# Weighted sums of a window attention for two pairs at a time, in slots 1 and 3 of a quad

## The reference

```python
xw  = windows(roll(norm(x)))                       # 7 x 7 windows: 49 tokens of 96
q, k, v = split(xw @ qkv_w + qkv_b)                # 12 heads of 8; layer 3: 4 heads of 24
attn = softmax(q * hd**-0.5 @ k.T + bias + mask)   # over 49 keys
out = (attn @ v) @ proj_w + proj_b                 # attn @ v: the weighted sums
x   = x + unroll(unwindows(out))
x   = x + mlp(norm(x))
```

## Time and profile before

| | |
|---|---|
| median of 3 runs | 7,912.68 us (7,911.06 to 7,913.54) |
| profiled execution, its own time | 7,913.45 us |
| its span, first to last instruction | 7,911.6 us |
| mean granted TensorE clock | 0.991 |
| busy TensorE / VectorE / ACT / GpSimd | 96% / 77% / 63% / 67% |

### The profile page before, as it was taken

The page is one execution under the profiler, slowest core; times in us unless marked ns, Lnnn a source line. Parts: engine busy times, 40 slices in busy tenths (PEclk is TensorE's granted clock), DMA queues, the critical chain, the costliest instruction groups (busy, mean ns, idle before and its releaser), DMA issues.

```text
span 7911.6 us, 312040 instructions
## 1 busy us (share of the span) xinstructions
PE 7632.4 (96%) x109686; PEld 5869.5 (74%) x109686; DVE 6090.9 (77%) x18297; ACT 5020.8 (63%) x8745; POOL 5284.7 (67%) x6553
## 2 busy tenths in 40 slices
PE   5999999999999999999999999999999999999998
PEld 4777777777777777777777777777777777777777
DVE  6877778767787877877878687786787878778677
ACT  3847657557784765745777475674577747567457
POOL 4956657567795765756789476675678857566566
PEclk9999999999999999999999999999999999999999
DMA  2101101010010110101011011010101101011010
GB/s 61 39 11 30 51 13 32 12 35 18 24 40 30 34 47 17 32 8 41 11 31 46 23 33 42 22 33 7 43 5 36 57 11 33 13 27 30 11 41 25
DMA packets 309910, 227.60 MB, mean 29 GB/s; under 512 B 217380, under 2 KB 305767, under 8 KB 306345
## 3 DMA queue, kind: packets, MB, share of 16 engines
q1 hardware_dynamic: 307858, 215.98, 10.2%
q10 hardware_dynamic: 1622, 6.13, 0.2%
HBM read 117.62 MB, written 104.37 MB: 28 GB/s over the span
## 4 chain that ended last, share of the span: by engine, by line
PE 80%; DVE 7%; issue 6%; DVEq 2%; POOL 2%; ACT 1%; POOLq 0%; ACTq 0%
PE ps L942 13%; PE ps L992 12%; PE ps L917 10%; PE ps L893 10%; PE ps L1035 8%; PE ps L1008 8%; PE ps L949 5%; PE ps L972 5%; PE ps L982 3%; PE ps L926 3%; DVE xn L1210 2%; DVE bst L1061 2%; PE ps L1022 2%; PE ps L873 1%; DVE x L1366 1%
## 5 line engine op out<-in xcount | busy, mean ns | idle before, releaser
L667 POOL TENSOR_TENSOR S<-S,mx 113x588 f32<-113x588 f32 (+1 forms) x2048 | 2066.8, 1009 | 1075.2 <-DVE mx L1261 1069.8
L773 ACT ACTIVATE S<-S 113x588 f32<-113x588 f32 (+1 forms) x2048 | 1251.5, 611 | 480.0 <-POOL S L667 465.3
L1259 DVE TENSOR_TENSOR S<-ps,bias 113x588 f32<-113x588 f32 (+1 forms) x1536 | 969.6, 631 | 611.5 <-PE ps L917 568.5
L1261 DVE TENSOR_REDUCE mx<-S 113x12 f32<-113x588 f32 (+1 forms) x2048 | 1359.6, 664 | 70.8
L802 ACT ACTIVATE PT<-ps 123x490 f32<-123x490 f32 (+1 forms) x2048 | 1059.4, 517 | 399.8 <-PE ps L992 395.2
L992 PEld LDWEIGHTS ps<-turn,S 113*123 113x123 f32 (+2 forms) x8704 | 1006.6, 158 | 386.2 <-issue 185.4
L1008 PEld LDWEIGHTS ps<-w,G 128*98 128x98 f32 x12288 | 1152.0, 168 | 158.9 <-issue 87.5
L992 PE MATMUL ps<-turn,S 113*123 113x113 f32 (+2 forms) x8704 | 1232.6, 266 | 13.7 <-ACT S L773 4.5
L1008 PE MATMUL ps<-w,G 128*98 128x96 f32 (+1 forms) x12288 | 1152.8, 250 | 0.0
L1035 PE MATMUL ps<-h,w 97*128 97x392 f32 x3072 | 1125.3, 503 | 9.1 <-ACT G L837 9.1
L942 PEld LDWEIGHTS ps<-Va,PT 123*49 123x49 f32 (+1 forms) x18432 | 815.4, 125 | 292.7 <-issue 243.9
(11 more groups left out here) (94 smaller groups left out, 11984.3 us busy)
## 6 DMA issues: line engine op xcount, KB each, us to landing
v_between<-Vd SPq DMA_DIRECT2D x384, 165.4 KB
Va<-v_between SPq DMA_DIRECT2D x768, 41.3 KB
Vb<-v_between SPq DMA_DIRECT2D x768, 27.6 KB
v_between<-Vd SPq DMA_DIRECT2D x128, 153.1 KB
Vl<-v_between SPq DMA_DIRECT2D x256, 76.6 KB
out_dram<-x SPq DMA_DIRECT2D x15, 1176.0 KB
x<-x_dram SPq DMA_DIRECT2D x14, 1176.0 KB
mask<-mask_dram SPq DMA_DIRECT2D x258, 37.5 KB
```

The costliest lines, as they stand in the source:

```text
L667: pool.tensor_tensor(v, v, m, ALU.subtract).then_inc(a_sub, 1)
L773: act.activation(S[:, e, 0:nh * N], S[:, e, 0:nh * N], ACT.Exp).then_inc(a_exp, 1)
L1259: dve.tensor_tensor(dst, scores, b, ALU.add).then_inc(a_bi, 1)
L1261: dve.reduce_max(mx[:, e, 0:nh], S[:, e, 0:n].rearrange("p (h k) -> p h k", k=N), axis=AX.X).then_inc(a_mx, 1)
```

## The change

The weighted sums become a function `weigh(par, pairs)`. TensorE calls it in slot 3 for pairs 0 and 1 of quad i, behind the waits for the weights of pair 1 (before: pair 0), the scaled output of quad i - 1 and the values; and in slot 1, after the queries, for pairs 2 and 3 of quad i - 1, behind the wait for the weights of its pair 3. Slots 0 and 2 have none. On VectorE the scaling moves from slot 2 to slot 1, and the four `bn_stats` from slot 1 to slot 3, right ahead of the four `bn_aggr`. The line of the value copy is not changed: it stays in slot 2, where the scaling stood ahead of it.

```diff
+                    def weigh(par, pairs):
+                        pieces = [blocks_of(nh, par, w) for w in range(2)]
+                        for p in pairs:
+                            for b in range(blocks):
+                                for w in range(2):
+                                    rows, _, h, v = pieces[w][b]
+                                    v = v[:, :, p]
+                                    out = Ops[ROW2 * w:ROW2 * w + N, p, h:h + v.shape[1], :]
+                                    last = pe.matmul(out, PT[0:rows, p, b, N * w:N * (w + 1)], v,
+                                                     start=(nh == 4 or b % 2 == 0), stop=True, skip_group_check=True)
+                        return last
...
-                        if on(-1) if s < 3 else on(0):
-                            wait(a_pte, i.pair(s - 3))
-                            p = (s + 1) % 4
-                            if s == 3:
-                                wait(a_o, i - 1)
-                                spread = spread_count(l, g, i, t)
-                                pe.wait_ge(s_vb[t], spread if i.static else pe.snap(spread))
...
-                            if s == 2:
-                                last.then_inc(a_pv, 1)
+                        if s == 3 and on(0):
+                            wait(a_pte, i.pair(1))
+                            wait(a_o, i - 1)
+                            spread = spread_count(l, g, i, t)
+                            pe.wait_ge(s_vb[t], spread if i.static else pe.snap(spread))
+                            weigh(t, (0, 1))
...
                         if s == 1 and on(1):
                             wait(a_res, i - 2)
                             project(queries_at(l, i), 0).then_inc(a_q, 1)
+                        if s == 1 and on(-1):
+                            wait(a_pte, (i - 1).pair(3))
+                            weigh(o, (2, 3)).then_inc(a_pv, 1)
...
-                        if s == 2 and on(-1):
+                        if s == 1 and on(-1):
                             wait(a_pv, i - 1)
...
-                        if s == 1 and on(-2):
+                        if s == 3 and on(-2):
                             wait(a_res, i - 2)
                             if not (i.static and i.index < 4):
                                 wait(a_mv, i - 4)
                             stats(i - 2, xb, (i - 2).index * QUAD, QUAD, t, a_bn)
-                        if s == 3 and on(-2):
                             aggregate(i - 2, QUAD, t, a_bn, a_agg)
```

## The result

The changed kernel takes 8,049.35 us (median of 4 runs, 8,047.37 to 8,053.61) where the kernel before takes 7,913.08: 136 us more, a ratio of 1.0173 [1.0156, 1.0191]. The forecast was 8,014, within 7,905 to 8,085. Part 1 of the page of the changed kernel, busy time, share of the span and instructions, against the earlier trace rows: TensorE has the same number of matmuls, and is busy for a smaller share of a longer span.

The account below looks back on a forecast made before the run. TensorE, busy nearly throughout, with pair 1's transposes waiting for their exponential, was taken as the bound. Per-quad terms 0.25 + 0.26 + 0.26 + 0.10, times 29 quads and 4 groups, gave +101 us: 8,014 us, range 7,905 to 8,085.

Parts of the forecast that it names:

- The late ST(3): Slot 0, layers 1 and 2: transposes of pair 3's exponentials wait 0.29 us because of GpSimd's power; +0.26 us per quad.
- The faster rival: Pair 3's exponential is ready in time, as GpSimd or ACT work 0.3 us sooner: 7,873 us; chance 0.12.
- Layer 0: ACT's xn delays pair 3's exponential, so its transposes wait; net +0.42 and +0.07 in the two quads, mean +0.25 us.
- slots 1 and 2 stay at 4.96 us together: Layers 1 and 2: pair 1's transposes still wait for their exponential, so these slots change by nothing.
- Entering the group from the projection: Slot 1: going from query projection to weighted sums costs 0.08 us, between nothing and 0.16.
- Layer 3: Slot 0's output projection waits for ACT's eviction of its input, taken at 0.18 us; +0.10 us per quad.
- a rival for layers 0 to 2 only: Slot 3's statistics and aggregation delay pair 0's add and the residual; the query projection waits: 8,084 us; chance 0.12.
- 0.28 us of cover: Slot 1: the query projection starts 3.25 us after pair 0's scores start, the residual ends at 2.97; no wait.
- VectorE's moves, costed at nothing: Scaling to slot 1, statistics to slot 3: no instruction added or removed; pair 0's add perhaps a tenth late, covered.
- The tie of the scaling: Scaled product ends about 3.5 us after pair 1's scores start, pair 2's scores end at 3.4; costed at nothing.
- The rule on drains: TensorE: mode changes per quad fall from 13 to 12, an estimated 41 us saved, some 7,872 us.
- One reading of the prediction: Kernel before, GpSimd: pair 3's subtraction starts at 712.32, where the power ends, not where its maximum lets it.

Follow-up runs that it names:

- the move of xn: Changed kernel with ACT making xn behind pair 3's exponential instead of ahead of it in layer 0: 8,020.13 us, 1.0136.
- The exchange of order: Changed kernel with slot 1's weighted sums of pairs 2 and 3 ahead of the query projection on TensorE: 8,001.54 us, 1.0113.
- the first experiment: Changed kernel with GpSimd's copy, sum and power behind pair 1's subtraction (slot 1) instead of pair 2's in layers 1 and 2: 8,015.86 us, 1.0131.

## Why the prediction was right, and where its size was off

- **The late ST(3) in layers 1 and 2**: right in its place, cause and size. Slot 0 was forecast at 2.8 and is 2.83; the wait was forecast at 0.29 and is 0.28. That GpSimd's power causes it is shown: with it elsewhere slot 0 is 2.48. The faster rival, that GpSimd would take that work sooner, did not happen.
- **Layer 0**: the waits were forecast at 0.45 and 0.10 (0.57 less a margin of 0.47), and are 0.47 and 0.12. Shown by the move of xn.
- **The mis-sized term: "slots 1 and 2 stay at 4.96 us together".** They take 5.07 in layers 0 to 2. Entering the group from the projection was priced well (0.85 from queries to weighted sums, 705.62 to 706.47, against 0.76 from queries to transposes in the kernel before, 705.81 to 706.57, and as much behind scores in layer 3 of the kernel with the groups in slots 0 and 2: 0.09). What was not priced is the exit: until then no ST stood right behind weighted sums, and ST(0) now runs 0.10 longer there. Slot 2, freed of its group, hides nothing any more, so the 0.10 goes on through ACT's eviction and pair 1's exponential to ST(1). 0.11 x 87 quads x 4 groups = 38 us, which is the whole gap between 8,014 and 8,049 and a little more. The exchange of order, which brings back 4.97 and 4.31, shows the cause.
- **Layer 3**: the wait for the output projection's input is 0.18, as taken. The wait for the residual, which the prediction priced as a rival for layers 0 to 2 only, is real here in every second quad: 0.22, or 0.11 per quad. Slot 3 gives 0.06 back (+0.18 where +0.24 was forecast), so +0.15.
- **"0.28 us of cover" for the query projection** was rightly computed from the residual's old time, but hung on the wait itself. Without the late ST(3) the cover is gone, and the first experiment met that. The forecast of the faster rival, 7,873, was wrong for this reason too.
- **VectorE's moves, costed at nothing**: right for the scaling, not for the statistics. The tie of the scaling is one: the product ends at 708.11 + 0.56 = 708.67, S(2) at 708.19 + 0.50 = 708.69, and pair 2's add starts at 708.80. With the statistics in slot 3, pair 0's add starts later in every second quad: 0.98 us behind S(0) instead of 0.61 in layer 0, 1.11 instead of 0.93 in layer 1, 1.25 instead of 0.79 in layer 3. The prediction allowed a tenth. The residual comes later with it: it ends 3.01, 3.15 and 2.65 behind S(0), before 2.76, 2.97 and 2.35. In layers 0 to 2 the wait at ST(3) covers that. In layer 3 it is the 0.22: with the statistics back in slot 1 the residual ends at most 2.38 behind S(0), and the query projection doesn't wait. At 0.11 per quad the term is 0.11 x 29 x 4 = 13 us. Still, neither move can be taken back.
- **The rule on drains.** The Trainium skill's page "TensorEngine Tiling (Array Packing)", section "Key Properties", says that a change of tiling mode drains TensorE. Counted alone it gave 7,872. The traces agree that such a change costs something between weighted sums and projections (0.08 to 0.09 at entry and exit), but scores cost 0.43 whatever follows, and transposes behind the group cost 0.10 more: the price depends on the neighbours. By the slots without waits, TensorE's own saving with that order is about 0.03 us per quad (slot 0 -0.57, slot 1 +0.65, slot 3 +0.46, slot 2 taken at -0.57); with the queries behind the group, slot 1 is +0.46 and the saving 0.22.
- **The sum of it**: the change saved TensorE next to nothing and made the slots more uneven. GpSimd's power, ACT's xn and the residual stood where the old lengths covered them.

One reading of the prediction was weaker than it says. In the kernel before, pair 3's subtraction starts at 712.32, where the power ends, but its maximum ends only 0.08 ahead of that, at 711.47 + 0.77 = 712.24, so these rows alone could not tell which of the two holds it. VectorE's timeline of the kernel before:

```profile
711.47 0.77 DVE L1261 TENSOR_REDUCE mx<-S 113x12 f32<-113x588 f32 x1
```

In the changed kernel maximum and subtraction are 0.77 apart, and the first experiment settles it.

## What to carry to other kernels

Before work is joined on a full engine, look at what the emptied slots fall back on: a slot, or a run of slots, is no shorter than the chain through the other engines that it covered. A wait that a change makes also covers waits behind it, so price the next one as if the first were gone; here the residual stood behind the exponential, and in layer 3 two evictions behind the residual; the joined groups paid, by 0.3%, only with four pieces of work moved. Put a group of another kind where the work behind it does not hang on the critical chain.

## What the runs showed of the hardware that was not expected

- Five transposes that start right behind a weighted-sum group take 0.69 us to the next scores, behind a projection that waits for nothing 0.59, after a wait 0.66 (changed kernel and the one with the groups ahead of the queries). Why they do is not settled by these runs.
- In every second quad of layer 3, VectorE stands idle for 0.58 us after the aggregation without a releaser, 0.16 in the other quad. The two quads are the two halves of the loop's body. In the longer gap the trace has a compare-and-branch of the loop's line in VectorE's sequencer, at 3708.78, which the other gap has not; that the branch takes this time was not tried by itself.
